# Contexts for the cross attention's scores: a second load in blocks that VectorE turns, in place of TensorE's transposes, with the last key as a column of its own

## The reference

```python
q = hidden_states @ Wq                      # hidden_states = layernorm(x)
k = encoder_hidden_states @ Wk              # encoder_hidden_states = ctx_768, 257 keys
v = encoder_hidden_states @ Wv
scores = jnp.einsum('bhsd,bhkd->bhsk', q, k) * scale
probs = jax.nn.softmax(scores, axis=-1)     # 16 heads, 257 keys
out = jnp.einsum('bhsk,bhkd->bhsd', probs, v)
out = out.transpose(0, 2, 1, 3).reshape(B, S, H * Dh) @ Wo + bo
```

## Time and profile before

| | |
|---|---|
| three runs | 1581.54, 1582.34 (median), 1584.12 us |
| span of the profiled execution | 1580.3 us |
| PE busy | 1543.1 us (98%), 13802 matmuls |
| weight loads busy | 1287.0 us (81%) |
| VectorE, ScalarE, GpSimd busy | 1066.2 (67%), 737.1 (47%), 371.2 us (23%) |
| context transposes (L640) | 384 matmuls |
| DMA queues | 36.9% of 16 engines' span, 210.74 MB |

### The profile page before, as it was taken

The page is one execution under the profiler, slowest core; times in us unless marked ns, Lnnn a source line. Parts: engine busy times, 40 slices in busy tenths (PEclk is TensorE's granted clock), DMA queues, the critical chain, the costliest instruction groups (busy, mean ns, idle before and its releaser), DMA issues.

```text
span 1580.3 us, 36115 instructions
## 1 busy us (share of the span) xinstructions
PE 1543.1 (98%) x13802; PEld 1287.0 (81%) x13802; DVE 1066.2 (67%) x2306; ACT 737.1 (47%) x1596; POOL 371.2 (23%) x225
## 2 busy tenths in 40 slices
PE   7999899999999999999999999999999999998989
PEld 6888788988999899888988898878878878786544
DVE  8766677677666766776667766657555664556788
ACT  5444656455545554555545554433123222224755
POOL 1000235343444344343434344400000000000000
PEclk9999999999999999999999999999999999999999
DMA  6898864341334223431434133250311311223022
GB/s 241 318 369 345 328 238 139 125 154 57 125 138 138 90 92 138 138 133 58 141 127 153 54 128 124 81 200 22 107 63 35 115 49 42 99 84 134 1 107 107
DMA packets 78958, 210.74 MB, mean 133 GB/s; under 512 B 5712, under 2 KB 31760, under 8 KB 76048
## 3 DMA queue, kind: packets, MB, share of 16 engines
q1 hardware_dynamic: 78864, 209.39, 36.9%
HBM read 140.42 MB, written 68.94 MB: 132 GB/s over the span
## 4 chain that ended last, share of the span: by engine, by line
PE 75%; issue 12%; DVE 8%; ACT 4%; DMA 0%; DVEq 0%; SPq 0%; ACTq 0%; POOLq 0%; POOL 0%
PE psum_o L694 13%; PE psum_s L671 7%; PE psum_q L671 7%; PE psum_o L1488 6%; PE psum_q L1528 6%; PE psum_q L1488 6%; PE psum_t L1560 6%; PE psum_o L559 5%; PE psum_o L709 5%; DVE qk L1092 3%; PE psum_t L682 3%; PE psum_t L640 2%; PE psum_s L1515 1%; PE psum_t L591 1%; PE psum_q L591 1%
## 5 line engine op out<-in xcount | busy, mean ns | idle before, releaser
L694 PE MATMUL psum_o<-pT,c_nat 128*128 128x512 f32 x1152 | 307.3, 403 | 3.4 <-issue 2.4
L694 PEld LDWEIGHTS psum_o<-pT,c_nat 128*128 128x128 f32 x1152 | 202.7, 189 | 38.7 <-DVE pT L957 3.6
L1304 POOL TENSOR_TENSOR c_nat<-c_raw,constants 128x768 fp32r<-128x768 f32 x64 | 93.8, 1466 | 560.1 <-PE psum_o L694 445.3
L1158 DVE TENSOR_SCALAR oT<-psum_o,c_last 128x512 f32<-128x512 f32 x192 | 143.7, 748 | 65.5 <-PE psum_o L694 65.5
L671 PE MATMUL psum_s<-cT,qk 128*128 128x256 f32 (+1 forms) x1152 | 167.7, 288 | 2.3 <-DVE cT L957 0.3
L671 PEld LDWEIGHTS psum_s<-cT,qk 128*128 128x128 f32 x1152 | 151.0, 189 | 11.3 <-DVE cT L957 5.2
L671 PE MATMUL psum_q<-cT,qk 128*128 128x256 f32 (+1 forms) x1152 | 152.8, 284 | 1.0 <-DVE qk L1092 1.0
L884 ACT ACTIVATE probs<-psum_s,nmax 128x257 f32<-128x257 f32 x128 | 61.1, 477 | 197.7 <-DVE nmax L1173 197.7
L671 PEld LDWEIGHTS psum_q<-cT,qk 128*128 128x128 f32 x1152 | 143.3, 190 | 4.0 <-issue 2.6
L957 DVE TENSOR_TENSOR pT<-psum_t,pT 128x512 fp32r<-128x512 f32 x128 | 87.8, 687 | 70.9 <-ACT pT L775 70.9
L1289 POOL TENSOR_TENSOR c_raw<-c_raw,last_row 128x768 f32<-128x768 f32 x64 | 120.3, 1881 | 29.5 <-DMA last_row<-in_ctx_dram 19.1
(11 more groups left out here) (295 smaller groups left out, 3118.2 us busy)
## 6 DMA issues: line engine op xcount, KB each, us to landing
qk_by_tile<-staged SPq DMA_DIRECT2D x32, 1536.0 KB, 10.1
raw<-qk_by_tile SPq DMA_DIRECT2D x16, 3072.0 KB, 12.3
c_raw<-in_ctx_dram SPq DMA_DIRECT2D x64, 384.0 KB, 3.3
last_row<-in_ctx_dram SPq DMA_DIRECT2D x64, 192.0 KB, 4.0
out_dram<-x_out SPq DMA_DIRECT2D x32, 256.0 KB, 2.0
x_res<-in_x_dram SPq DMA_DIRECT2D x16, 256.0 KB, 2.7
x_in<-out_dram SPq DMA_DIRECT2D x4, 1024.0 KB, 8.5
x_all<-out_dram SPq DMA_DIRECT2D x1, 4096.0 KB, 13.3
```

What stands on the lines that cost most here:

```text
L694: i = pe.matmul(ps[:], c_nat[(b - 1) % 2][:, part, k, m * P:(m + 1) * P], pT[:, moving, k, :], start=(k, part, moving) == (0, 0, 0), stop= ...
L1158: nc.vector.tensor_scalar(oT[:, m, :, (b - 1) % 4, :], ps[:].rearrange("p (s q) -> p s q", q=SQ), c_last[:, (b - 1) % 2, m:m + 1], None, A ...
```

## The change

Each context is loaded a second time, as blocks of 32 keys by 96 features (`load_blocks`: four DMAs of 32 partitions, 256 pieces of 384 bytes each, into one buffer `c_blk`). One VectorE instruction turns all 32 by 32 blocks (`dve_turn`), so that feature 3p+c lies on partition p in chunk c; `Wk`'s rows are loaded in the same order. ScalarE writes the last key as columns 256 and 257 (`act_last_column`), then the high part of the whole turned context in one instruction (`act_context_high`); VectorE then makes the low part in one instruction, in place (`dve_context_low`). The last key is no longer subtracted for the scores, so all score matmuls take 258 columns. The transposes on TensorE, their PSUM units and the copies out of PSUM go. To make room, `last_row` has one buffer (`load_ctx` waits for the previous subtraction, `s_sub`), and `x_out` is merged into `x_res` (its load for the next tile waits for the store, `s_out`).

```diff
@@ pe_scores @@
-            keys = SKP if section == "first" or (b, rg) == (0, 3) else 2 * P
+            if rg == 0:
+                pe.wait_ge(s_ctlo, 4 * t + (b + 1))
             for c in range(KC):
-                if rg == 0:
-                    wait_chunk(pe, t, b, section, c)
                 for part, moving in PARTS:
-                    m = pe.matmul(ps[:, 0:keys], qk[:, part, rg, c, b, :], cT[b % 2][:, moving, c, 0:keys],
+                    m = pe.matmul(ps[:, 0:SKP], qk[:, part, rg, c, b, :], cT[b % 2][moving][:, c, :],
@@ pe_cross_tile: both calls of pe_ctxT go @@
@@ act_cross_tile, steps after the first @@
                 exp(b, 0)
+                if after:
+                    act_last_column(act, 4 * t, b + 1)
...
+                if after:
+                    act_context_high(act, 4 * t, b + 1)
                 exp(b, 3)
-                if after:
-                    ctxT(b, 0)
-                    ctxT(b, 1)
...
+        def act_context_high(act, batch, ahead):
+            act.wait_ge(s_lastcol, batch + (ahead + 1))
+            act.wait_ge(s_turn, batch + (ahead + 1))
+            nc.scalar.activation(cT[ahead % 2][0][:], cT_raw[ahead % 2][:], ACT.Copy).then_inc(s_cthi, 1)
+        def dve_turn(dve, batch, ahead):
+            dve.wait_ge(s_blk, 64 * batch + 64 * (ahead + 1))
+            nc.vector.transpose(cT_raw[ahead % 2][:, :, 0:2 * P].rearrange("p c (k n) -> p c k n", n=KEYS),
+                                c_blk[:].rearrange("p k (i c) -> p c k i", c=KC)).then_inc(s_turn, 1)
+        def dve_context_low(dve, batch, ahead):
+            dve.wait_ge(s_cthi, batch + (ahead + 1))
+            nc.vector.tensor_tensor(cT[ahead % 2][1][:], cT_raw[ahead % 2][:], cT[ahead % 2][0][:].bitcast(F32),
+                                    ALU.subtract).then_inc(s_ctlo, 1)
@@ dve_cross_tile, steps after the first @@
                 row_max(b, 2)
                 inverse(b, 1)
+                if after:
+                    dve_turn(dve, 4 * t, b + 1)
...
                 if after:
-                    ctxT(b, 0)
-                    ctxT(b, 1)
+                    dve_context_low(dve, 4 * t, b + 1)
                 norm(b, 2)
                 norm(b, 3)
                 dve_attended(dve, t, b, 1, section)
...
                     dve_x_out(dve, t, section)
-                if after:
-                    ctxT(b, 2)
                 dve_attended(dve, t, b, 2, section)
@@ sync queue @@
+        def load_blocks(sp, batch, ahead):
+            if not isinstance(batch, int) or batch + ahead:
+                sp.wait_ge(s_turn, batch + ahead)
+            keys = ctx_of(batch, ahead)
+            for f in range(4):
+                quarter = keys[:, 0:2 * P, f * QUARTER:(f + 1) * QUARTER]
+                sp.dma_start(c_blk[KEYS * f:KEYS * (f + 1), :, :],
+                             quarter.rearrange("a (k n) d -> n (a k) d", n=KEYS)).then_inc(s_blk, 16)
         def load_ctx(sp, batch, ahead):
+            if not isinstance(batch, int) or batch + ahead:
+                sp.wait_ge(s_sub, batch + ahead)
@@ sp_cross_tile @@
             for b in range(4):
+                if b == 0 and section != "second":
+                    load_x_res(sp, t)
                 if more or b < 2:
+                    load_blocks(sp, 4 * t, b + 2)
                     sp.wait_ge(s_nat, 4 * t + (b + 1))
                     load_ctx(sp, 4 * t, b + 2)
@@ sp_project_all, after the stores of the project stage @@
+            load_blocks(sp, 0, 2)
             sp.wait_ge(s_nat, 2)
             load_ctx(sp, 0, 3)
             load_qk(sp, 0, 1)
+            load_blocks(sp, 0, 3)
```

More of the change, by code:

```diff
@@ L80, in cross_units @@
             u.append((("WO",), "q1"))
-        if not (section == "last" and b == 3):
-            u += [(("CT", b, c), ("t0", "t1")[c % 2]) for c in range(3)]
     return u
@@ L90, in split_only @@
 def split_only(units):
-    return [u for u in units if u[0][0] in ("XT", "Q", "WK", "CT", "PT", "W")]
+    return [u for u in units if u[0][0] in ("XT", "Q", "WK", "PT", "W")]
 def split_only2(units):
@@ L256, in build_kernel @@
         cT1_at = sb.at
-        cT1 = sb("cT1", [P, 2, KC, SKP], F32R)
+        cT1 = [sb(f"cT1_{part}", [P, KC, SKP], F32R) for part in ("low", "high")]
         c_nat1 = sb("c_nat1", [P, 2, 2, DC], F32R)
@@ L288, in build_kernel @@
         cT0_at = sb.at
-        cT0 = sb("cT0", [P, 2, KC, SKP], F32R)
+        cT0 = [sb(f"cT0_{part}", [P, KC, SKP], F32R) for part in ("low", "high")]
         c_nat0 = sb("c_nat0", [P, 2, 2, DC], F32R)
@@ L726, in pe_cross_tile @@
         def pe_cross_tile(pe, t, section):
-            begun, more = section != "first", section != "last"
+            begun = section != "first"
             for b in range(4):
@@ L733, in pe_cross_tile @@
                 pe_scores(pe, t, b, 1, section)
-                if not before:
-                    pe_ctxT(pe, t, b, section, (0, 1))
                 pe_scores(pe, t, b, 2, section)
@@ L739, in pe_cross_tile @@
                         pe_wv(pe, t, n, section)
-                if not before:
-                    pe_ctxT(pe, t, b, section, (2,))
                 pe_scores(pe, t, b, 3, section)
@@ L744, in pe_cross_tile @@
                     pe_pv(pe, t, b, 0, section)
-                if before and (more or b < 3):
-                    pe_ctxT(pe, t, b, section, (0, 1))
-                if before:
                     pe_pv(pe, t, b, 1, section)
@@ L938, in act_cross_tile @@
                     act_qk_high(act, t + 1, 3)
-                if after and (b < 3 or begun):
-                    ctxT(b, 2)
         def act_cross_tail(act):
@@ L1126, in dve_project_all @@
                 else:
[L1127 to L1129 removed]
+                    dve_turn(dve, 0, 0)
                 for j in range(4, 8):
@@ L1164, in dve_x_out @@
             dve.wait_ge(s_xb, t)
-            dve.wait_ge(s_out, 16 * t)
-            nc.vector.tensor_tensor(x_out[:], ps[:], x_res[:], ALU.add).then_inc(free, 1)
+            nc.vector.tensor_tensor(x_res[:], ps[:], x_res[:], ALU.add).then_inc(free, 1)
         def dve_cross_tile(dve, t, section):
@@ L1408, in sp_project_all @@
                     if (s, j) == (GROUPS - 1, 4):
-                        full(sp, project(("CT", "start", 2)))
+                        load_blocks(sp, 0, 1)
                         sp.wait_ge(s_nat, 1)
@@ L1426, in sp_project_all, with load_x_res @@
             sp.dma_start(x_res[:], rows(x_rows, 0)).then_inc(s_xres, 16)
+            load_blocks(sp, 0, 4)
             sp.wait_ge(s_nat, 4)
             load_ctx(sp, 0, 5)
+            load_blocks(sp, 0, 5)
+        def load_x_res(sp, t):
+            sp.wait_ge(s_out, 16 * t)
+            sp.dma_start(x_res[:], rows(x_rows, t - 1)).then_inc(s_xres, 16)
         def sp_cross_tile(sp, t, section):
@@ L1448, in sp_cross_tile @@
             sp_x1(sp, t, section)
-            sp.dma_start(x_res[:], rows(x_rows, t)).then_inc(s_xres, 16)
         def sp_x1(sp, t, section):
@@ L1457, in sp_x1 @@
                 dst = x1_dram[bass.ds((t - 1) * P, P), :]
-            sp.dma_start(dst, x_out[:]).then_inc(s_out, 16)
+            sp.dma_start(dst, x_res[:]).then_inc(s_out, 16)
         def rows(ap, t, ahead=0):
```

130 lines of the change are left out of this document (51 added, 79 removed).

## The result

| | before | after |
|---|---|---|
| median | 1582.19 us (4 runs) | 1573.35 us (4 runs, 1573.09 to 1574.5) |
| span of the profiled execution | 1580.3 | 1571.4 |
| matmuls recorded | 13802 | 13421 |

The ratio is 0.994, 95% interval 0.9926 to 0.9954: faster by 9 us, where 28 were forecast. The time lies inside the range, near its end, and the gain is a third of the one predicted.

The account below looks back on a forecast made before the run. TensorE was taken to bound the kernel. The span was 1580.3 - 41.6 - 5.9 + 2.3 + 13.5 + 3 = 1551.6 us; the median lies 2.1 us above the profiled span, giving 1554 us, range 1537 to 1576.

Parts of the forecast that it names:

- the third rival: VectorE's turn is slow reading every third element, 1.8 us, delaying boundary and short steps: 1566 to 1579, chance 0.14.
- The bound and the place of the new wait: TensorE sets the loop's pace; a new wait for VectorE comes ahead of the boundary's first `pe_pv`, about 0.9 us.
- What goes: TensorE's context transposes go, 0.65 us for each of 64 contexts, 41.6 us; 0.39 us at 15 boundaries, 5.9 us, too.
- The boundary wait: TensorE's new wait for VectorE at each tile boundary, taken as 0.9 us, +13.5 us over 15 boundaries.
- the walk: Boundary queues followed by instruction: VectorE's second low part ends at 650.26, TensorE arrives at 649.51, 0.75 us waited.
- The columns: Score matmuls of 258 columns for 256 on TensorE, some 2,000 of them, cost +2.3 us, bounds 0 and 18.
- the sum: The forecast's terms dealt out to the loop: each tile's period changes by -1.95 us.
- Tile 0: Start-up stretch: late blocks and a clock dip against waits TensorE loses, +3 us, bounds -5 and +9.
- The turn: VectorE's `STREAM_TRANSPOSE` of 768 elements in each step takes 0.98 us.
- the fourth rival: The blocks' small DMA pieces land late, VectorE and TensorE wait in the loop: slower, 1611 us, chance 0.07.
- the shorter bound: The four block loads of a context land after 5.0 us without queueing, 7.2 us if they queue.
- The low part and ScalarE's copy: In each step VectorE's low part of 774 takes 0.95 us; ScalarE's copy takes 0.8 us, costing nothing on average.

Follow-up runs that it names:

- the hole: The changed kernel with VectorE's turn moved in each step from behind row group 1's inverse to behind row group 0's row maximum: 1575.55 us, ratio 0.9954.
- ScalarE's move: On top of the hole, ScalarE's context copy in b=3 behind qk's second high part, and VectorE's context low part later in tile 0: 1567.22 us.
- The first experiment: The changed kernel with SyncE's tile 0 queue reordered, context 3's blocks ahead of `load_qk`, context 4's ahead of wo, wv, bo and x_res: 1562.19 us.
- the fourth experiment: The changed kernel with score matmuls at 256 columns, 258 only in tile 0 and for b=0, row group 3: 1571.43 us, ratio 0.9917.
- the third experiment: The changed kernel with the turn reading neighbours instead of every third element, nothing else adapted: 1568.86 us, ratio 0.9902.
- the third move: The first experiment plus, from tile 1, the hole and ScalarE's move; next tile's first row maximum ahead of `x_out`, b=0 turn moved back: 1543.81 us, the fastest version.

## Why the prediction was right or wrong

The forecast was 1554 and the time 1573.35. It lies inside the stated range, but in the part that was put there for the third rival (1566 to 1579) and mostly not by that rival's mechanism: reading neighbours brings 4.5 us by the medians, while the stretch of tile 0 came 12.3 us above its forecast.

- **The bound and the place of the new wait: right.** TensorE sets the period, the wait stands ahead of the first `pe_pv` after the boundary, VectorE's second low part of the probabilities releases it, and the score groups there are at 1.10 us again (1.46 before).
- **What goes: right.** 381 matmuls fewer are recorded, 384 gone and three added. Groups of three `pe_pv` are 18 matmuls in 4.08 to 4.30 us; with their transposes they took 4.81 to 4.85 before. By these starts, less the waits inside, the transposes were worth 2.7 us a tile, forecast 2.6.
- **The boundary wait: right in kind, small.** 1.09 against 0.9. VectorE came to its second low part's end 20.97 us after the start of b=3's scores (581.71 to 602.68), 0.29 later than the walk's 20.68; the turn, 1.22 us and not 0.98, is 0.24 of that. TensorE needs 0.20 more from that end to its first matmul, which the walk had not, and comes 0.26 later than walked itself, so that 0.98 and not 1.24 are waited at first.
- **A wait not seen: 0.2 us a tile.** In b=3 the first weight load of `wo` waits for ScalarE's fourth exponential, which empties the bank. The list of waits (us, times, longest) has it:

```profile
PEld psum_q L698 <- ACT probs L861: 4.5, 13, 0.4
```

  The last gap of `pe_pv` before it is 0.08 longer and the group of `wo` 5.58 us in place of 5.46. The prediction called the copy "nothing on average", then named that exponential as queued behind it and took this as covered, by looking at the next scores only. It is the queue's order in one step that counts, not the average; the hole and ScalarE's move took these waits away (5.45).
- **The columns:** 0.20 us a tile on TensorE by starts (without the waits 17.63 became 17.83), forecast 0.15; worth 0.13 when taken away. Together with the last two points, 0.19 + 0.20 + 0.05 less 0.11 on the transposes = 0.33, against 0.32 that the period misses (49.74, where 51.37 less the 1.95 of the sum is 49.42).
- **Tile 0: the step that failed.** "+3 us, bounds -5 and +9" was the term, and the stretch from the first scores to wv of tile 1 came out 12.3 us above the forecast that holds it, so the term measured about +15, over its bound and over the 10 us named as the point of being wrong. The queue of SyncE was followed for context 3 only: `load_qk` ahead of the blocks was seen, and put at a wait of 3 to 5 us, measured 6.83. Context 4 was not followed at all: its blocks stand behind four loads whose issues take 6.3 us, and came 3.47 late. TensorE waited 6.26 and 4.13 us behind these two. The first experiment takes 10.2 of the 12.7 us back by order alone; what the other 2.6 are stays open. The clock was priced as one dip of 1.7 us, while it stood at the lower level for 23.8 us, but by the fourth experiment's kernel the waits and not the clock set this stretch. (The 0.66 of the earlier trace rows isn't a level: it is the mean of 5 us, 3.4 of them at 0.50.)
- **The turn:** 1.22 for 0.98. The forecast took the trace's row of neighbours for a read of every third element, and argued that a float32 element is read by itself in either case, so that the stride would cost nothing; the third experiment shows that it costs 0.26 us. Read as neighbours the turn takes 0.96, which is the forecast's 0.98 to 0.02. The Trainium skill, page "SBUF — State Buffer", section "Door 1: The DMA port swizzle", says that reads of SBUF are at full rate when each 16-byte line is hit twice or more, and also that float32 may be strided by 4 for free. At a stride of 12 bytes a line is hit 1.3 times, so the first sentence agrees with the 27% and the second doesn't.
- **Late blocks (the fourth rival): false in the loop.** The fourth issue leaves 1.5 us after the first and lands 2.4 later, 3.9 in all, under the 5.0 of the shorter bound, and no tile of the loop has VectorE waiting for them. The Trainium skill, page "DMA: Bandwidth & Descriptors", section Specifications, wants transfers of 512 bytes or more for line rate. This case's landings, 2.4 us for 384-byte and 2.0 us for 192-byte pieces, show nothing of it; its packets do in part, at 1.35 and 1.85 times the time of a 1536-byte one for a byte. Blocks that land late are also what happened in tile 0, but by the queue ahead of them and not by the pieces.
- **The low part and ScalarE's copy:** 0.949 and 0.854 us, forecast 0.95 and 0.8. The collision with GpSimd named for tile 0 came (1.995 us once).

## What to carry to other kernels

Follow each queue that a load is put in through the start-up as well as through the loop, instruction by instruction, and add the issue times of what stands ahead: two exchanges there were worth more than the whole change had brought. A wait has a second releaser right behind the first (VectorE, then ScalarE, then VectorE's order again), so a move is worth what the next one allows, and only the third move gave the loop back to TensorE. When a value that starts a long chain of two engines, such as a first row maximum, stands behind work that nobody waits for yet, change these places (here together with the turn of b=0). And read a total that meets its forecast stretch by stretch: one did here with 2.6 us lost and 1.7 gained that were not in its sum.

## What the runs showed of the hardware

A `STREAM_TRANSPOSE` of 128x768 float32 took 1.217 us when it read every third element and 0.959 when it read neighbours. Loads of 256 pieces of 384 or 192 bytes landed in 2.4 and 2.0 us, 3.5 for 256 pieces of 1536; a single packet of them took 22, 15 and 65 ns. And the granted clock stood at 0.50 for 23.8 us up to wv of tile 1 in the changed kernel, for 17.1 in the fourth experiment's, and for 6.8 in the fastest one. Nearly the same first waits of TensorE went with different clocks: 1.87 and 0.66 us with a low stretch that starts at 194.1, 1.89, 0.66, 1.03 and 2.35 with none there, 1.60, 0.66, 1.03 and 2.35 with one of 3.4 from 199.7. What in the waits decides it stays open, and the first of these differences cost no time, since a slower TensorE waited less.
